# Two of four row tiles of a feed-forward input are centred and weighed on GpSimd instead of VectorE

## The reference

```python
def _layernorm(x, axis=-1, eps=1e-05):
    return (x - mean(x)) / sqrt(var(x) + eps)

def rmsnorm(x, g):
    return x * rsqrt(mean(x * x) + 1e-6) * g

def activation_quant(x):
    scale = 127.0 / maximum(max(abs(x)), 1e-5)
    return clip(round(x * scale), -128, 127) / scale

def bitlinear(x, w, g):
    return activation_quant(rmsnorm(x, g)) @ weight_quant(w).T

u = bitlinear(_layernorm(h), w_in, g_in)      # 192 -> 1024
up, gate = split(u, 2)
h = h + bitlinear(silu(gate) * up, w_out, g_out)   # 512 -> 192
```

## Time and profile before

| | us |
|---|---|
| median of 3 runs | 2611.77 (2610.54 to 2612.75) |
| the profiled execution | 2611.97 |
| its span | 2610.1 |
| VectorE busy | 1907.7 (73%) |
| TensorE busy | 2240.0 (86%) |
| GpSimd busy | 1022.0 (39%) |

### The profile page before, as it was taken

One profiled execution on the slowest core, in us unless ns is written; L12 is line 12 of the kernel. 1 busy time (PEld: TensorE's weight loads), 2 busy tenths in 40 slices (PEclk: granted clock), 3 DMA queues, 4 the chain that ended last, 5 costly groups with the idle time before them and its releaser, 6 DMA issues. The chain is left out here.

```text
span 2610.1 us, 45380 instructions
## 1 busy us (share of the span) xinstructions
PE 2240.0 (86%) x14046; PEld 1629.5 (62%) x14047; DVE 1907.7 (73%) x5361; ACT 1586.8 (61%) x2815; POOL 1022.0 (39%) x1128
## 2 busy tenths in 40 slices
PE   8999999999999699999992799992578888676665
PEld 4444444444444588888882799992567776554444
DVE  5777777777774589889883566663657777789997
ACT  2444444444444488888872577773678774667777
POOL 1100100100000156666665477776555543345443
PEclk9999999999999799999995899996788998877777
DMA  2000000000000323333333788887666640000001
GB/s 60 1 19 13 1 19 13 1 9 1 1 0 1 106 51 75 72 72 74 73 73 114 227 257 257 263 257 150 85 82 92 80 55 1 17 22 27 27 27 32
DMA packets 114523, 183.09 MB, mean 70 GB/s; under 512 B 14338, under 2 KB 84327, under 8 KB 114079
## 3 DMA queue, kind: packets, MB, share of 16 engines
q0 software_dynamic: 74816, 86.34, 17.6%
q1 hardware_dynamic: 39556, 94.85, 11.4%
HBM read 64.46 MB, written 64.39 MB: 49 GB/s over the span
## 5 line engine op out<-in xcount | busy, mean ns | idle before, releaser
L213 ACT ACTIVATE prob<-pscore 128x896 f32<-128x896 f32 x336 | 308.0, 917 | 423.8 <-PE pscore L295 423.8
L420 DVE TENSOR_REDUCE pmax<-ppre 112x1 f32<-112x512 f32 x656 | 424.0, 685 | 162.6 <-PE ppre L262 162.5
L309 PE MATMUL pout<-prob,xkey 128*64 128x448 f32 x1344 | 328.3, 567 | 0.4 <-ACT prob L213 0.4
L262 PE MATMUL ppre<-xh,yh 49*112 49x512 f32 x656 | 291.2, 446 | 7.8 <-DVE pmax L420 4.2
L1578 POOL DMA_INDIRECT rows_out<-yb,home3b x252 | 246.8, 979 | 115.7 <-issue 60.7
L195 POOL CAST yh<-ynext 113x448 fp32r<-113x448 f32 x28 | 17.2, 614 | 667.6 <-DVE pmax L420 639.5
L262 PEld LDWEIGHTS ppre<-xh,yh 49*112 49x112 f32 x656 | 112.8, 172 | 239.9 <-issue 103.5
L737 POOL DMA_INDIRECT rows_in<-xr,idx x224 | 215.8, 964 | 117.9 <-DVE idx L1269 54.0
L295 PE MATMUL pscore<-yh,xh 49*128 49x448 f32 x700 | 241.2, 422 | 0.4 <-DVE yh L440 0.4
L1885 POOL TENSOR_TENSOR sums<-rows,gout 112x512 f32<-112x512 f32 x112 | 143.0, 1287 | 231.8 <-DVE rows L2521 228.6
L295 PE MATMUL pscore<-yh,xl 49*128 49x448 f32 x700 | 202.7, 364 | 0.0
(11 more groups left out here) (398 smaller groups left out, 6502.7 us busy)
## 6 DMA issues: line engine op xcount, KB each, us to landing
wd<-down SPq DMA_DIRECT2D x63, 512.0 KB, 3.0
xb<-rows_in SPq DMA_DIRECT2D x63, 455.0 KB
sums<-rows_out POOLq DMA_DIRECT2D x56, 336.0 KB, 6.2
h<-brow POOLq DMA_DIRECT2D x28, 336.0 KB, 5.2
h<-gambet POOLq DMA_DIRECT2D x28, 336.0 KB, 4.9
out<-sums SPq DMA_DIRECT2D x28, 336.0 KB, 2.8
rows_in<-zero SPq DMA_DIRECT2D x15, 455.0 KB, 6.1
rows_out<-yb,home3b POOLq DMA_INDIRECT x252
```

What stands on the lines that cost most here:

```text
L213: nc.scalar.activation(prob[j % 3][:, :, :], pscore[j % 2][:, :, 0:CH], ACT.Exp).then_inc(exped, 1)
L262: pe.matmul(out[:, :], yh1[rows, q * T:(q + 1) * T], xh[b % 2][rows, block * 512:(block + 1) * 512], start=True, stop=True, tile_position= ...
L309: mm = pe.matmul(pout[i * LO:(i + 1) * LO, 0:CH], xkey[b % 2][:, 2 * j + i, :], prob[j % 3][:, i, :], start=(j == 0), stop=(i == 1 and j = ...
L420: nc.vector.reduce_max(pmax[:, q, 2 * block + half:2 * block + half + 1], bank(u, depth), AX.X).then_inc(pre_max, 1)
```

## The change

GpSimd gets a `weigh_in` for the row tiles 2 and 3: a subtraction of the mean, spread over the 192 columns, and a multiplication by `gin`, spread over the two tiles, both 112 x 384 and the second in place. It begins when the last reading of `xg` is over (`xr_out`), and signals `xw_out`. VectorE keeps row tiles 0 and 1, and its `largest_in` waits for both. In GpSimd's stream chunks 0 and 1 stand ahead of the loop, chunk 2 inside iteration 0, and chunk g+2 at the head of iteration g.

```diff
+            def weigh_in(g):
+
+                if g == 0:
+                    pool.wait_ge(F["fac_in"], 1)
+                else:
+                    pool.wait_ge(F["xr_out"], g)
+                if (g + 1) * TPC > HEAD:
+                    pool.wait_ge(F["fac_in"], 2)
+                some = xg[:, 2:TPC, :]
+                cols = slice(g * TPC + 2, (g + 1) * TPC)
+                nc.gpsimd.tensor_tensor(some, h[:, cols, :], mean[:, cols].unsqueeze(2).broadcast_to([T, 2, D]),
+                                        ALU.subtract).then_inc(F["xc_out"], 1)
+                pool.wait_ge(F["xc_out"], g + 1)
+                nc.gpsimd.tensor_tensor(some, some, gin[:].unsqueeze(1).broadcast_to([T, 2, D]),
+                                        ALU.mult).then_inc(F["xw_out"], 1)
+
...
             factor5(0, slice(0, HEAD))
             pool.wait_ge(F["gin_in"], 32)
+            weigh_in(0)
+            weigh_in(1)
             for g in range(NC):
+                if g + 2 < NC and g:
+                    weigh_in(g + 2)
                 weigh(g, 0)
+                if g == 0:
+                    weigh_in(2)
                 weigh(g, 1)
                 root_of(g)
...
             def weigh_in(g):
 
-                for q in range(TPC):
+                for q in range(2):
                     t = g * TPC + q
...
             def largest_in(g):
                 dve.wait_ge(F["xg_out"], g + 1)
+                dve.wait_ge(F["xw_out"], g + 1)
```

More of the change, by code:

```diff
@@ L1772, in attention_and_ffn_phase @@
                   "sg_out", "y_out", "yg_out", "ssq_out", "r2_in", "r2_out", "yq_out", "ytr_mm", "yT_out", "o_mm",
-                  "o_out", "stored", "dvec", "dvec2", "xg_out", "am_out", "fac_in", "fac_out", "scaled", "d2_out",
+                  "o_out", "stored", "dvec", "dvec2", "xg_out", "xw_out", "xc_out", "am_out", "fac_in", "fac_out", "scaled", "d2_out",
                   "xr_out", "yr_out", "s2_out", "ya_out", "am2_out")
```

## The result

| | before | changed |
|---|---|---|
| median, 20 runs each | 2612.0 us (2602.1 to 2618.4) | 2619.4 us (2609.8 to 2630.0) |
| ratio, 95% interval | | 1.0035 (1.0022 to 1.0048) |
| profiled execution, span | 2610.1 | 2625.3 |
| VectorE, sum of the steady part | 218.0 of 233 | 221.1 of 233 |

The changed kernel is slower by 0.35%, some 9 us (the two medians are 7.4 us apart). That is outside the 0.2% which the forecast (+3.2 us) named as no change; the time lies in the range, and the place is the one foreseen. The profiled execution is one of the slower ones of its kernel.

A forecast was written before the change was run, and what follows sets the result against it. It took the chain of waits between TensorE and VectorE (13.65 us a period) as the bound; 2.9 + 1.0 + 0.35 + 0.3 + 1.0 - 2.35 = +3.2 us on 2611.97 gave 2615.2 us, range 2609 to 2624.

The forecast's parts named there:

- Steady part, 0 us: Iterations 9 to 25: VectorE's weighing ends ahead of a wait for TensorE, so shortening it saves nothing; bounds 0 to 0.3 a period.
- one between the pair and L1885, one between the two L1885: Steady period: where VectorE's two remaining weighings fit between GpSimd's instructions, done by 2496.6, at worst 2498.2.
- L2513 ahead of the pair: Steady period: after xr_out VectorE's rounding starts before GpSimd's two weighing instructions, 0.04 against 0.13 to 0.14 us.
- The first rival: Slower: GpSimd's weighing gets in front of L2513, 0.9 us in nearly every iteration, +23 us, some 2638; chance 5%.
- The pair, 2 x 0.99 us: GpSimd's two new 112x384 instructions per chunk take 0.99 us each, 2.1 from start to end; bounds 0.95 and 1.27.
- The first wait, +2.9 us: Start, chunk 0: VectorE's maximum waits for GpSimd's weighing queued behind the power, delaying TensorE's query and key products by 2.9 us.
- The second chunk, +1.0: Start, chunk 1: VectorE's maximum waits for GpSimd's weighing, delaying L2383 and TensorE's map products by 1.0 us.
- Third chunk: Start, chunk 2: GpSimd's weighing pushes one L1885 against VectorE's two L2479, +0.35 us, bounds 0 and 1.0.
- Iterations 4, 5, 6, -0.65 each: Early iterations where VectorE runs without a gap to L2361: the shorter weighing saves 0.65 us each, 1.95 in all.
- TensorE's clock, +1.0 us: Start: the clock may fall at TensorE's new 2.8 us hole; +1.0, bounds 0 and 2 there, as much again behind.
- The rival with 29%: Slower: map products also run at 1.2 GHz, or spread operands slow GpSimd's weighing; +5.5 to +12 us, some 2620; 29%.
- rival E: Follow-up forecast, start: the clock falls only with chunk 1's stall as well; chunk 0's wait alone costs +3 us; no chance stated.

The follow-up runs named there:

- half weighed: Kernel before, with row tiles 2 and 3 weighed by no engine from chunk 3 on: 2608.1 us against 2610.4, ratio 0.9995.
- the hole alone: Kernel before, VectorE's first maximum held by a repeated 12-column power on GpSimd, no weighing moved; run twice: 2612.6 us (1.0015) and 2613.3 us (1.0016).
- first pair only: Changed kernel with GpSimd weighing two row tiles in chunk 0 alone, VectorE all others: 2613.1 us against 2609.8 before, ratio 1.0016.
- start only: Changed kernel with GpSimd weighing two row tiles in chunks 0 to 2 alone: 2615.9 us against 2609.9 before, ratio 1.0031.
- loop only: Changed kernel with GpSimd weighing two row tiles from chunk 3 on alone: 2611.9 us against 2609.9 before, ratio 1.0006.
- pair first: Changed kernel with GpSimd's weighing of chunk 0 put ahead of the 64-column power: 2608.3 us against 2609.9 before, ratio 0.9997.

## Why the prediction was right in its place and short in its size

- *Steady part, 0 us.* Held: 13.65 us a period, and half weighed shows that even free removal gives nothing. The wait was to be 1.3 us; it is 0.56. The step that failed is "one between the pair and L1885, one between the two L1885": L1885 follows the pair with no gap and was first, and each weighing waits out one L1885. The weighings end at 2512.56, in the time of before 2497.4, halfway between the 2496.6 taken and the 2498.2 of the worst case, and that fits into the wait.
- *L2513 ahead of the pair.* Held: L2536 started at 2507.47, L1897 at 2507.51, and L2536 took 0.56 as before. It was the pair's first piece that took 1.20 instead of 0.83. The first rival is out.
- *The pair, 2 x 0.99 us.* 0.83 and 0.99 where VectorE leaves it alone. Why the subtraction is the quicker one, no run shows.
- *The first wait, +2.9 us.* +2.86, hole 2.62.
- *The second chunk, +1.0.* L2508 came 22.51 us after the statistics instead of 19.01, of which 2.86 were there: +0.64. Third chunk +0.36 for +0.35. Iteration 8: +0.04 for +0.3.
- *Iterations 4, 5, 6, -0.65 each.* The two of them with the clock high show it, 15.89 to 15.90 us for 16.55; the third had a low clock, 19.33.
- *TensorE's clock, +1.0 us.* This is the term that was mis-sized. Its bounds were 0 and 2 on the last products and as much again behind. The first held in the changed kernel's two profiles: the last products kept 2.4 GHz in one, and in the other their fall made the first rounding 1.8 us later. The second didn't: the map products went at 1.2 GHz, and the stretch between the first two roundings took 26.0 and 24.3 us instead of 16.6. Less the 0.64 of the second chunk, that is 7.0 to 8.8 us for a bound of 2. The map products are on the path with 13.7 of 15 us busy, and that row should have set the upper bound: at half the clock they cost most of their own length. The rival with 29% had the price, +5.5 to +12. The measured 2619.4 lies outside the forecast's own 2612 to 2617; it is in the stated range because the larger part of this rival had been put into it.

What is shown of the clock and what isn't: of thirteen profiles, six had the full wait at the start, and in five of them the clock was low in the map products; seven had no wait or a short one, and in one of these it was low. These are single executions. The record also has the mean granted clock of every execution, and there the wait alone leaves no mark. The median of these means is 0.911 or 0.912 for the kernel before in each of the three groups of experiments, 0.911 and 0.912 in the two runs of the hole alone (24 executions) and 0.912 with the first pair only. It is 0.908 in start only and 0.909 in the 32 executions of the changed kernel. Such a median of twelve scatters by 0.001 to 0.002 (loop only has 0.910, half weighed 0.9095, pair first 0.913), so 32 executions weigh more here than twelve. As far as these medians go, the lower clock comes with the wait for the first pair and the later pairs together, as rival E had it, and not with the wait by itself. Why, no run shows.

How much of the median this is can be estimated only. In the 91 executions of the kernel before, 0.001 less mean clock went with 1.25 us more time. By that slope the 0.002 to 0.004 that the changed kernel and start only lack against the kernel before are 2 to 5 us. The direct terms of the changed kernel are 2.86 + 0.64 + 0.36 less some 2, so 2 us; together that is 4 to 7, for a difference of the medians of 7.4 us and a ratio that says 9. The hole alone measured +3 in twenty-four runs, the first pair alone +3 to +4, start only +6 to +8. That leaves 3 to 5 us between the first pair alone and the three pairs of the start, of which 1.0 is direct. The intervals of these two are some 9 us wide each, and no run held the clock, so the share of the clock stays open.

## What to carry over

Work that is moved to an idle engine goes behind what is queued there: look for the longest instruction ahead of it at the first use, not only at the steady place; here two exchanged lines took the whole loss back. Before an engine's load is cut, look for its next wait behind the cut; if there is one, fill it with work from beyond it (0.3% here) rather than shorten what lies ahead of it. And where a new hole opens ahead of a stretch in which TensorE is the path, price the stretch at the low clock, all of it, and give that case a chance of its own: the kernel with the hole alone had the mean clock of before over its 24 executions.

## What had not been expected of the hardware

- The clock fell to 1.2 GHz in the changed kernel and stayed there for 54.6 us, of which TensorE was busy 48.8; in the kernel with the hole alone it kept 2.4 GHz behind a hole of 3.12 us in one execution and fell behind one of 1.46 in another.
- GpSimd's 112x384 subtraction of one number a row took 824 ns, against 992 for the multiplication by a row of 192 numbers that is used twice.
- Beside the same two L1885, two VectorE weighings that began 0.17 us behind the first L1885 took 2.65 us (1.31 and 1.42), and four that began 1.08 us behind it took 2.41.
